# A cross-attention and MLP kernel: probabilities turned by way of DRAM and VectorE instead of on TensorE, the product with v and the output projection moved to the slot after

## The reference

```python
# layer 0, x_c = x, x_s = ctx
Mn = Wn @ inorm(x_c) + bn ; Mm = Wm @ inorm(x_s) + bm        # 128 x 512
A  = softmax(Mn.T @ Mm, axis=-1)                             # 512 x 512
x  = Wo @ (Ml @ A.T) + bo + x_c ; Ml = Wl @ x_s + bl
# layer 1, 16 heads of width 32
q = ln(x) @ q_w + q_b ; k = ctx @ k_w + k_b ; v = ctx @ v_w + v_b
P = softmax(q k^T * scale, masked)                           # 16 heads of 128 x 128
h = (P v) @ cproj_w + cproj_b + x
out = h + gelu(ln(h) @ fc_w + fc_b) @ proj_w + proj_b        # inner width 2048
```

## Time and profile before

| | |
|---|---|
| median of three runs | 3122.23 us |
| the profiled execution | 3121.42 us, span 3119.6 us |
| TensorE busy | 3067.8 us (98%) |
| VectorE busy | 1950.8 us (63%) |
| ScalarE busy | 1350.4 us (43%) |
| GpSimd busy | 817.7 us (26%) |
| granted clock | 0.994 of full speed, mean of the span |
| DMA | 147.54 MB, 15.9% of 16 engines |

### The profile page before, as it was taken

How to read it: one execution, slowest core, us unless ns; L and a number is a source line. 1 busy time by engine, 2 the same in 40 slices (tenths; PEclk the granted TensorE clock), 3 DMA queues, 4 the chain that set the end, 5 groups by cost and what they waited for, 6 DMA issues and landing times. The chain is left out here.

```text
span 3119.6 us, 54886 instructions
## 1 busy us (share of the span) xinstructions
PE 3067.8 (98%) x18551; PEld 2558.2 (82%) x18551; DVE 1950.8 (63%) x3961; ACT 1350.4 (43%) x3954; POOL 817.7 (26%) x742
## 2 busy tenths in 40 slices
PE   7999999999999999999997999999999999999999
PEld 5888888888888888888886788888888888888887
DVE  7888888888888888888885533333333333333332
ACT  4666666666666666666665211111111111111111
POOL 4444444444444444444443100000000000000000
PEclk9999999999999999999998999999999999999999
DMA  4111111111111111111112211111111111111110
GB/s 121 46 51 50 50 51 53 52 55 53 52 50 50 50 50 50 50 50 50 50 38 73 92 32 41 41 40 40 40 32 22 40 33 34 40 40 40 40 27 14
DMA packets 231920, 147.54 MB, mean 47 GB/s; under 512 B 142912, under 2 KB 176192, under 8 KB 231872
## 3 DMA queue, kind: packets, MB, share of 16 engines
q1 hardware_dynamic: 231872, 146.91, 15.9%
HBM read 97.57 MB, written 33.55 MB: 42 GB/s over the span
## 5 line engine op out<-in xcount | busy, mean ns | idle before, releaser
L1173 ACT ACTIVATE gl<-pre,fc_bias 128x512 f32<-128x512 f32 x256 | 176.6, 690 | 1119.4 <-PE pre L1258 1119.4
L1212 DVE CAST hT_hi<-gl 128x512 fp32r<-128x512 f32 x256 | 109.1, 426 | 837.7 <-ACT gl L1173 837.7
L627 ACT ACTIVATE rows<-bank,negmax 128x128 f32<-128x128 f32 x1024 | 362.9, 404 | 89.5 <-DVE negmax L808 89.5
L1256 PE MATMUL pre<-yT_lo,rest_hi 128*128 128x512 f32 x768 | 298.8, 389 | 0.0
L1257 PE MATMUL pre<-yT_hi,rest_lo 128*128 128x512 f32 x768 | 298.8, 389 | 0.0
L1258 PE MATMUL pre<-yT_hi,rest_hi 128*128 128x512 f32 x768 | 298.8, 389 | 0.0
L1256 PE MATMUL acc<-rest_lo,hT_hi 128*128 128x512 f32 x768 | 298.8, 389 | 0.0
L1257 PE MATMUL acc<-rest_hi,hT_lo 128*128 128x512 f32 x768 | 298.8, 389 | 0.0
L1258 PE MATMUL acc<-rest_hi,hT_hi 128*128 128x512 f32 x768 | 298.8, 389 | 0.0
L517 POOL TENSOR_TENSOR rows<-rows,rsum 128x512 f32<-128x512 f32 x256 | 259.0, 1043 | 18.7 <-DVE rsum L702 18.7
L872 PEld LDWEIGHTS bank<-ident,rows 128*128 128x128 f32 x2048 | 232.6, 141 | 21.3 <-ACT rows L627 3.7
(11 more groups left out here) (158 smaller groups left out, 7322.6 us busy)
## 6 DMA issues: line engine op xcount, KB each, us to landing
x_in<-in_x SPq DMA_DIRECT2D x64, 256.0 KB, 2.6
ctx_in<-in_ctx SPq DMA_DIRECT2D x64, 256.0 KB, 2.9
blocks<-in_ctx SPq DMA_DIRECT2D x256, 64.0 KB, 1.9
small<-in_x SPq DMA_DIRECT2D x64, 256.0 KB, 3.3
hidden<-hid SPq DMA_DIRECT2D x64, 256.0 KB, 2.0
rows<-hidden SPq DMA_DIRECT2D x16, 1024.0 KB, 5.4
out<-rows SPq DMA_DIRECT2D x64, 256.0 KB, 2.0
stage<-y SPq DMA_DIRECT2D x240, 64.0 KB, 2.1
```

The lines of the kernel that those rows point to most:

```text
L627: act.activation(probs[:, r, c, :], by_chunk(S1_BANK[r])[:, c, :], ACT.Exp, bias=negmax1[:, r, c:c + 1], accum_out=sum1[:, r, c:c + 1]).th ...
L1173: act.activation(gl[:, i % 2, :], pre[i % 2][:], ACT.Gelu_apprx_tanh, bias=mlp.fc_bias[:, i:i + 1]).then_inc(gelu_done, 1)
L1256: pe.matmul(out, a_hi, b_lo, start=first, stop=False)
```

## The change

What it does:

- The probabilities are no longer transposed on TensorE. SP writes them to a tensor in DRAM, `p_turn`, by four DMAs in pieces of 32 floats (`write_probs`), and reads them back as `p_blocks`, with the 32x32 blocks in their places (`read_probs`). VectorE transposes within the blocks (`turn_probs`), four instructions of 128x512.
- The product with v belongs to b4 and stands right after m; the output projection stands behind U; `hid` is made and stored later in the same slot.
- GpSimd normalises in the slot in which the exponentials are made, at its end, partly behind ctxT_lo.
- The scaling of A and the cast normed_hi go from VectorE to ScalarE. v_sb moves to the next slot, behind m_lo; ctx's turn moves ahead of x1; kT moves ahead of the reciprocals.
- The order of k turned and v is exchanged on TensorE, and the banks are given out anew.
- `p_blocks` is the first half of `stage`. The halves of `stage` are exchanged for the MLP's weights (`half_of`), and the second of the MLP's first two weight loads waits for the last turn.

The core of the diff:

```diff
+    p_blocks = stage[:, 0, :, :]
+    p_turn = nc.dram_tensor("p_turn", [4, P, T], F32, kind="Internal").ap()
...
+    M_BANK = (4, 7)
     PV_BANK = 5
+    C_BANK = 3
+    AT_BANK = S1_BANK = (0, 1, 2, 3)
+    XN_BANK = Q_BANK = V_BANK = 6
+    S0_BANK = (4, 7, 5, 0)
+    U_BANK = 1
+    OUT0_BANK = 2
+    QT_BANK = 3
+    K_BANK = 4
+    KT_BANK = 7
...
 # SP
+            def write_probs(e):
+                if e.has_before(1):
+                    after(pT_set, (e + -1).nth(4, 4))
+                after(probs_set, e.nth(4, 4))
+                for d in range(4):
+                    sp.dma_start(p_turn[d].rearrange("p (h b) -> p h b", b=32),
+                                 mlp.rows[:, 1, :, :].rearrange("p r (c d b) -> p d (r c) b", d=4, b=32)[:, d])\
+                      .then_inc(p_written, 16)
+            def read_probs(e):
...
+                after(p_written, e.nth(64, 64))
+                for d in range(4):
+                    sp.dma_start(p_blocks[32 * d:32 * (d + 1), :, :],
+                                 p_turn[d].rearrange("(q p) n -> p q n", p=32)).then_inc(p_blocks_in, 16)
...
+                if (s + -3).exists():
+                    write_probs(s + -3)          # first in SP's slot, before x_in, ctx_in, x_res, mask
...
+                if (s + -3).exists():
+                    read_probs(s + -3)           # then the loads of blocks, then the store of hid
 # ScalarE
+                if b4.exists():
+                    act.wait_ge(outT_done, b4.nth(1, 1))      # after m_hi
+                    act.activation(flat(outT_hi), bank[PV_BANK][:], ACT.Copy).then_inc(outT_hi_set, 1)
...
+                if b0.exists():
+                    act.wait_ge(rsum0_set, b0.nth(1, 1))      # after the copy of q, before that of k
+                    for t in range(DC):
+                        act.activation(A[:, t, :], A[:, t, :], ACT.Identity,
+                                       scale=rsum0[:, t:t + 1]).then_inc(a_scaled, 1)
...
+                if b2.exists() and b2.has_before(1):
+                    act.wait_ge(p_written, b3.nth(64, 64))
                 exp1(0)
                 exp1(1)
+                exp1(2)
...                                                            # ctxT_hi
-                exp1(2)
                 exp1(3)
 # VectorE, after m_lo and the last reciprocal
+                if b2.exists():
+                    dve.wait_ge(v_done, b2.nth(1, 1))
+                    if b4.exists():
+                        dve.wait_ge(outT_done, b4.nth(1, 1))
+                    dve.tensor_tensor(v_sb[:, b2.parity, :], bank[V_BANK][:], v_bias[:], ALU.add).then_inc(v_set, 1)
...
 # VectorE, the end of a slot: negmax1 (4), kT, then
+                sum1_reciprocal(b2, 0)
+                if b3.exists():
+                    dve.wait_ge(p_blocks_in, b3.nth(64, 64))
+                turn_probs(0)
+                turn_probs(1)
+                sum1_reciprocal(b2, 1)
+                turn_probs(2)
+                turn_probs(3)
                 sum1_reciprocal(b2, 2)
 # TensorE
+                if b2.exists():
+                    pe.wait_ge(kT_set, b2.nth(1, 1))          # before m
...
+                if b4.exists():
+                    pe.wait_ge(pT_set, b4.nth(4, 4))          # after m: product with v
...
                 if b2.exists():
                     pe.wait_ge(x1n_set, b2.nth(1, 1))
+                    pe.wait_ge(v_set, b2.nth(1, 1))
                     turn(bank[XN_BANK], lambda c: x1n[:, c * P:(c + 1) * P], xnT_turned)
...
-                if b3.exists():
-                    pe.wait_ge(exp1_done, b3.nth(16, 16))
-                    for r in range(4):
-                        pe.wait_ge(probs_set, b3.nth(4, r + 1))
-                        turn(bank[PT_BANK[r]], lambda c: probs[:, r, c, :], pT_turned)
```

More of the change, by code:

```diff
@@ L331, in attention_pass @@
         probs_set = sem("probs_set")
-        pT_turned = sem("pT_turned")
-        pT_copied = sem("pT_copied")
+        p_written = sem("p_written")
+        p_blocks_in = sem("p_blocks_in")
+        pT_set = sem("pT_set")
         outT_done = sem("outT_done")
@@ L474, in slot @@
                     load_blocks(e)
+                e = s + -4
+                if e.exists():
+                    after(hid_set, e.nth(1, 1))
+                    sp.dma_start(hidden[e.number], hid[:, e.parity, :]).then_inc(hid_stored[e.parity], 16)
             def load_for_mlp():
@@ L618, in slot @@
                     act.activation(k_sb[:], bank[K_BANK][:], ACT.Copy).then_inc(k_copied, 1)
-                if b3.exists():
-                    act.wait_ge(outT_done, b3.nth(1, 1))
-                    act.activation(flat(outT_hi), bank[PV_BANK][:], ACT.Copy).then_inc(outT_hi_set, 1)
+                if ahead.exists():
+                    for i in range(2):
+                        act.wait_ge(normed_set, ahead.nth(2, i + 1))
+                        act.activation(normed_hi[:, i, :], normed[:, i, :], ACT.Copy).then_inc(normed_hi_set, 1)
                 def exp1(r):
@@ L644, in first_weights @@
                 act.wait_ge(v_done, B)
[L645 to L649, removed]
+                for c in range(STAGE):
+                    mlp.upper_half(act, mlp.first_hi[:, 0, c, :], 0, c)
+            slots(act, slot, {1: lambda: upper_halves(V_W), LAST - 1: first_weights})
+            for c in range(STAGE):
+                mlp.upper_half(act, mlp.first_hi[:, 1, c, :], 1, c)
         @block.vector
@@ L687, in prepare_q @@
                 dve.wait_ge(q_bias_done, 1)
[L688 removed]
+                dve.tensor_tensor(q_bias[:], bank[3][:, 0:DC], vecs[:, 2, :], ALU.add).then_inc(q_bias_set, 1)
                 dve.wait_ge(q_bias_set, 1)
@@ L784, in slot @@
                                           in_rstd[:, i:i + 1], ALU.subtract, ALU.mult).then_inc(normed_set, 1)
-                    for i in range(2):
-                        dve.wait_ge(normed_set, ahead.nth(2, i + 1))
-                        dve.tensor_copy(normed_hi[:, i, :], normed[:, i, :]).then_inc(normed_hi_set, 1)
                 if b2.exists():
@@ L864, in prepare_q_bias @@
                     for c in range(DC):
-                        last = pe.matmul(bank[2][:, m:m + 1], stage[:, Q_W % 2, c, m * P:(m + 1) * P],
+                        last = pe.matmul(bank[3][:, m:m + 1], stage[:, Q_W % 2, c, m * P:(m + 1) * P],
                                          vecs[:, 1, c:c + 1], start=(c == 0), stop=(c == DC - 1))
@@ L930, in slot @@
                     prepare_q_bias()
+                if b4.exists():
+                    if not b4.has_before(1):
+                        pe.wait_ge(w_lo_set[C_W], 4)
+                    pe.wait_ge(outT_lo_set, b4.nth(1, 1))
+                    project(bank[C_BANK], outT_hi, outT_lo, C_W, cproj_done)
                 if b2.exists():
@@ L953, in slot @@
                     if b0.exists():
[L954 removed]
+                        pe.wait_ge(exp0_done, b0.nth(4, 1))
                     project(bank[K_BANK], ctxT_hi, ctxT_lo, K_W, k_done)
[L956 to L964 removed]
                 if b2.exists():
@@ L984, in slot @@
                 if b1.exists():
+                    pe.wait_ge(k_copied, b1.nth(1, 1))
+                    turn(bank[KT_BANK], lambda c: k_sb[:, c * P:(c + 1) * P], kT_turned)
                     if not b1.has_before(1):
```

190 lines of the change are left out of this document (82 added, 108 removed).

## The result

The changed kernel took **3273.98 us** (median of four runs, 3271.43 to 3278.27) against 3121.91 for the kernel before in the same runs: a ratio of **1.0489** (95% interval 1.0471 to 1.0507). It is slower. Forecast were 3214 us, in a range of 3110 to 3420. The profiled execution has a span of 3271.9 us, 152.3 more than before.

A forecast was written before the change was run, and what follows sets the result against it. The prediction took TensorE, without holes, to bound the kernel before, and a loop through all engines after. Sixty slots +82, slot 3 -1.4, end +12 gave +92, so 3214 us; 80% range 3110 to 3420.

The forecast's parts named there:

- The loop: Attention slot: S1, exp1, m_hi, m_lo, v_sb, x1n, S0, U, cproj, q, out0, x1, qT, S1 take 27.1 us against 25.77.
- the branch of v_sb: After S1: the longer branch; v_sb behind m_lo is seen at 9.93, so TensorE stands 1.1 us before x1n's turn.
- the branch of pT: After S1: VectorE's turns are seen at 6.1, so TensorE stands 1.45 us before the product with v.
- the last step: Slot's end: qT, seen 0.75 after its start, comes at 25.9; S1 stands 0.4 more and ends at 27.13.
- VectorE's sum: VectorE's work in one attention slot, 22.1 us before, was to stay at 22.3 us after the change.
- The bounce: Probabilities through DRAM: writes of 6.6 us just fit, x_res landing at 21.9 where x1 wants it at 22.2.
- the rival: Bound by the bounce: writes take W, more than 7 us, x_res sets x1, slot 20.6 + W; 18%.
- The end: From the last S1 to the MLP's first transpose: 38 us instead of 25.7, +12.
- The slots with fewer blocks before it come out equal by the same orders: Slots with fewer blocks ahead of the last batch: no added time.
- The start: Slot 3, without product with v or projection: loop 2.7 shorter, 24.4 us, so -1.4.
- The MLP is unchanged.: The MLP part after the attention: no term in the forecast's sum.
- the rivals: For the slot: bound by the bounce 18%, TensorE rules 8%, a shorter loop 8%, a longer loop 8%.

The follow-up runs named there:

- a2_vsb: The changed kernel with v_sb put ahead of m_lo on VectorE: 3213.44 us, 1.0295 of the kernel before.
- a3_turns: The changed kernel with the first two of VectorE's four turns put ahead of the reductions of S1: 3282.29 us, 1.052 of the kernel before.
- a4_write2: The changed kernel with the probabilities written a second time, to a tensor nobody reads, ahead of the loads on SP: 3642.68 us, 1.1673 of the kernel before.
- b1_before_pad: The kernel before with 161 semaphore increments at the start of TensorE's MLP part: 3177.94 us in a single run.
- a1_pad: The changed kernel with 95 semaphore increments on TensorE's queue at the start of the MLP part: 3255.23 us, 1.0431 of the kernel before.

## Why the prediction was right, and what was wrong in it

**The loop: right, though its waits were sized roughly.** Counted from the end of S1 (817.49), by my steps and by the rows above: first exponential 0.88 and 0.92; m_lo 7.72 and 7.74; the turn of x1n 9.93 and 9.95; x1 22.2 and 22.3; qT 25.2 and 25.28. All three holes of TensorE have the releasers named. By the profile they are 0.79, 1.19 and 0.71, 2.7 us together, where I had 1.45, 1.1 and 0.4 and wrote 3.3 for the sum. The profile shows a matmul as 0.39 long though the next one follows 0.23 behind it, so it shows each hole 0.16 short: counted from when the next matmul was due they are 0.96, 1.41 and 0.87. a2_vsb shows that the branch of v_sb rules and a3_turns that the branch of pT doesn't. **Mis-sized: the last step.** "qT is seen 0.75 after its start": no row of before shows that figure, and S1 started 1.03 behind it (842.77 to 843.80). With 0.1 from x1, which started 22.3 behind S1 and not 22.2, the slot was 27.5 instead of 27.13. Over the slots the loop's term was 101 instead of 82. VectorE's sum was put 1.1 too high (22.3, measured 21.2); for a loop that runs through waits that had no effect.

**The bounce: right, from a term that was too high.** GpSimd was done at 10.35 (10.4). I took 6.6 us for the writes, between 5.5 and 11.1; they took 4.30 to issue, below my lower end. That holds for a queue that was empty: the second set of a4_write2, issued while the first is on its way, took 6.26, near my 6.6. "DMA busy 0.46 of 13 us, so 6.0 us at full use" was no measure of full use: the same figure is 1.61 while a4_write2 does nothing but write (827 to 833). The way to x_res was longer instead: 2.1 behind x_in, not 1.2, and 3.6 to land, not 3.3. Together 20.8 for my 21.9 (x_res landed at 810.8, S1's end in that slot 27.5 ahead of 817.49). The bounce was priced at 20.6 + W a slot in the rival; its own terms (15.3 + W to x1, 4.9 from x1 to S1's end) make 20.2 + W. The Trainium skill ("DMA: Bandwidth & Descriptors", Specifications) has transfers below 512 B done as read-modify-write and short of line rate, and gives no cost; doubled, which was my estimate, it was 13 us of writes and a slot of 33 to 34. The trace shows 4.30 us of issue and about 8 to the last landing for the 8192 pieces, so that price did not fall due. That they move slowly is seen: 173 GB/s from 827 to 833 in a4_write2, and 359 from 835 to 836, when other transfers follow. Nothing in these runs tells how long wider pieces would have taken to DRAM.

**The end: right for the last batch, wrong ahead of it.** From the last S1 to the MLP I had 38 us and it was 38.3. "The slots with fewer blocks before it come out equal by the same orders" was argued only, and they cost 5.6 more.

**The start: wrong sign, its size not firm.** I took off 1.4 for slot 3, at 24.4 us; from m_lo to m_lo it took 29.4 (80.94 to 110.30), against 25.4 before. TensorE waits in it for v_sb and qT, longer than in the loop, and the granted clock falls to its lower level (1.2 GHz) for some microseconds at the end of each of the two waits:

```profile
83.16 1.08 PE L929 MATMUL bank<-ident,x1n 128*128 128x128 f32 x4 [2.12 <-DVE v_sb L776]
...
100.31 0.61 PE L1030 MATMUL bank<-mask_less,masked_bf 1*128 1x512 bf16 x4 [2.65 <-DVE qT L862]
```

The second of the two stretches is seen in these windows, before and after:

```profile
100.00:105.00 5.00, 5.00 (x26) 4.12 (x25) 3.25 (x8) 5.00 (x28) 1.71 (x2) 1.00 0.09 26
```

```profile
100.00:105.00 5.00, 4.69 (x47) 4.17 (x48) 3.75 (x6) 1.85 (x10) 2.56 (x2) 0.66 0.21 44
```

Up to slot 5 it is 5.0 more in this pair of profiles. But b1_before_pad, whose attention is that of before, came there at 135.6 instead of 132.4, and a1_pad, whose attention is that of after, at 136.0 instead of 137.4. So single executions differ by 3 us there, and no run divides the 5.0.

**The failed step: "The MLP is unchanged."** 28.3 of the 60 us by which the time exceeds the forecast. Its instructions are unchanged; their place in the program isn't, and a1_pad and b1_before_pad show that the place alone makes and unmakes the stops. I gave no reason for the zero: the instruction queue's row on the page before (28 packets) was there, and had no term in the sum. The error in sum: loop +19, start +6, slots with fewer blocks +6, end +1, MLP +28: 60.

So the time lies inside the range, and the sign and the mechanism were right, but about half of the excess came from a place where I expected nothing. 3274 is outside 3190 to 3240, which I had given to the forecast's own mechanism; it lies inside 3110 to 3420 only because that range was drawn wide for the rivals, which is luck.

## What to carry to other kernels

Where engines hand work around in a loop, an instruction's place in an engine's written order can be worth more than work taken off the busiest engine: one move of v_sb gave 60 us, one of qT 48, while 1.75 us a slot taken from TensorE shortened the slot by 0.3 us at best, and only with those moves. An idle row names what came last, not what it costs: x1 waited 2.2 us for x_res, and the load made earlier changed no slot, because out0 came at the same time. Price a part of a program that "isn't touched" too: compare its own window and the instruction queue's packets before and after, for a shift of some instructions cost 28 us here and 48 idle ones gave it back. And a longer pipeline pays at its ends: what a bounce hides in the steady state was 12 us in the open after the last batch.

## What the runs showed of the hardware that was not expected

- A TensorE loop of 1582 instructions ran with six stops of 3.1 to 3.8 us (changed kernel and b1_before_pad) or without any, depending on how many instructions stood ahead of it (with stops behind 3872 and 4384, without behind 4223, 3967 and 3920). The stops go with 53 to 55 more packets of 16 KB on the instruction queue.
- A semaphore increment on TensorE that does nothing else took 0.17 us (16.3 us for 95), a one-column matmul with its weight load 0.4 (9.6 us for 24).
- 1 MB written to DRAM in 8192 pieces of 128 B was issued in 4.30 us and landed about 8 us after its first issue; a second such set right behind the first took 6.26 to issue. Such writes alone moved 173 GB/s, with the DMA share of the profile at 1.61, so that share is no fraction of a full use.
- In a slot of a4_write2 TensorE stood from 836.8 to 842.7, and its granted clock was 0.50 from 839.8 to 846.6; the scores in this stretch took 2.25 us instead of 1.22.
